# Spectral stage of a two-layer block: the mixing weights of each filter built on GpSimd, with one broadcast product and running sums

## The reference

```python
def _compute_spectral(u, sigma, phi, Mpp, Mpm):
    U_plus, U_minus = _stu_conv(phi, u, PADDED_SL)   # causal convolution with K = 16 filters
    s = sigma ** SIGMA_POW
    out = jnp.einsum('btkd,k,kde->bte', U_plus, s, Mpp)
    out = out + jnp.einsum('btkd,k,kde->bte', U_minus, s, Mpm)
    return out
...
for i, frac in enumerate((1, 2, 4, 8)):
    xi = x[:, :T // frac]
    si = _stu(xi, sigma, phi, M_u[i], M_phi_plus[i], M_phi_minus[i])
    si = jnp.pad(si, ((0, 0), (0, T - si.shape[1]), (0, 0)))
    outs.append(si)
...
return jnp.sum(stacked * weights, axis=-1)
```

## Time and profile before

| | us |
|---|---|
| median of 3 runs | 6255.01 |
| lowest and highest run | 6253.27 and 6257.36 |
| profiled execution, its own time | 6258.71 |
| span of the profiled execution | 6256.9 |
| TensorE products busy in the span | 5702.8 (91%) |
| VectorE busy | 4472.1 (71%) |
| ScalarE busy | 3169.5 (51%) |
| GpSimd busy | 2832.3 (45%) |

### The profile page before, as it was taken

The page is one execution under the profiler, slowest core; times in us unless marked ns, Lnnn a source line. Parts: engine busy times, 40 slices in busy tenths (PEclk is TensorE's granted clock), DMA queues, the critical chain, the costliest instruction groups (busy, mean ns, idle before and its releaser), DMA issues. The chain is left out here.

```text
span 6256.9 us, 128558 instructions
## 1 busy us (share of the span) xinstructions
PE 5702.8 (91%) x41691; PEld 5079.1 (81%) x41691; DVE 4472.1 (71%) x6306; ACT 3169.5 (51%) x6029; POOL 2832.3 (45%) x1695
## 2 busy tenths in 40 slices
PE   7899999999888999999997659999999899999998
PEld 5688888888667888888885538888888788888887
DVE  2699999999618999999995645555555555555554
ACT  2699888988638998899885221111111111111110
POOL 1699999999608999999994300000000000000000
PEclk8899999999989999999999879999999999999999
DMA  2455555555415555555554147776766666777765
GB/s 96 113 141 144 139 142 143 142 143 137 121 56 136 143 143 139 138 145 145 141 138 124 43 128 156 149 152 147 153 151 149 164 140 151 148 154 149 149 150 143
DMA packets 1098945, 858.32 MB, mean 137 GB/s; under 512 B 305622, under 2 KB 1021238, under 8 KB 1064374
## 3 DMA queue, kind: packets, MB, share of 16 engines
q1 hardware_dynamic: 1097974, 844.72, 55.8%
q10 hardware_dynamic: 720, 10.49, 0.4%
HBM read 811.50 MB, written 43.55 MB: 137 GB/s over the span
## 5 line engine op out<-in xcount | busy, mean ns | idle before, releaser
L726 POOL TENSOR_TENSOR read<-state,c_wide 128x1024 f32<-128x1024 f32 x1024 | 2419.3, 2379 | 213.5 <-DVE state L762 127.3
L762 DVE TENSOR_TENSOR_SCAN state<-decay,carry,p_drive 128x512 f32<-128x512 f32 x1792 | 2140.5, 1258 | 104.0 <-PE p_drive L540 57.2
L658 ACT ACTIVATE decay<-step,a_neg 128x512 f32<-128x512 f32 x2048 | 1398.1, 717 | 223.8 <-DVE state L762 214.3
L1747 PE MATMUL p_y<-window,x_high 128*128 128x256 f32 x7936 | 1495.9, 286 | 0.0
L1811 ACT COPY term_blocks<-p_s 128x256 f32<-128x256 f32 x832 | 310.5, 373 | 2157.2 <-PE p_s L1747 2157.2
L1747 PEld LDWEIGHTS p_y<-window,x_high 128*128 128x128 f32 x7936 | 1243.6, 191 | 0.0
L1747 PE MATMUL p_y<-window,x_low 128*128 128x256 f32 x3968 | 1132.5, 285 | 0.0
L553 PE MATMUL p_y<-ident,read 128*128 128x128 f32 x8192 | 1064.1, 273 | 13.0 <-ACT y_tok L672 3.7
L542 PE MATMUL p_drive<-diag_b,xu_tok 128*128 128x128 f32 x8192 | 1002.7, 276 | 1.3 <-DVE state L762 1.3
L542 PEld LDWEIGHTS p_drive<-diag_b,xu_tok 128*128 128x128 f32 x8192 | 959.2, 193 | 1.6 <-DVE state L762 1.6
L553 PEld LDWEIGHTS p_y<-ident,read 128*128 128x128 f32 x8192 | 925.2, 141 | 25.5 <-issue 21.7
(11 more groups left out here) (257 smaller groups left out, 5443.7 us busy)
## 6 DMA issues: line engine op xcount, KB each, us to landing
c_wide<-c_scratch SPq DMA_DIRECT2D x256, 1024.0 KB, 4.8
window<-taps_scratch SPq DMA_DIRECT2D x576, 257.0 KB, 6.4
diag_b<-diag_scratch SPq DMA_DIRECT2D x256, 512.0 KB, 4.1
window<-taps_scratch SPq DMA_DIRECT2D x768, 129.0 KB, 5.1
window<-taps_scratch SPq DMA_DIRECT2D x128, 513.0 KB, 7.3
window<-taps_scratch SPq DMA_DIRECT2D x64, 385.0 KB, 6.2
gate_scratch<-gate_out SPq DMA_DIRECT2D x16, 512.0 KB, 3.1
gate_in<-gate_scratch SPq DMA_DIRECT2D x8, 1024.0 KB, 6.3
```

Source lines behind the costliest of these rows:

```text
L658: act.activation(decay[:, n % 2, t, :], step[:, c.parity, t, :], ACT.Exp, scale=m.a_neg[:, DT2 * c.k + t, n:n + 1]).then_inc(s["decay"], 1)
L726: pool.tensor_tensor(read[:, n % 4, :, :], state[:, n % 4, :, :], wide, ALU.mult).then_inc(s["read_out"], 1)
L762: dve.tensor_tensor_scan(flip(state[:, n % 4, t, :], c), flip(decay[:, n % 2, t, :], c), flip(p_drive[:, n % 2, t, :], c), 0.0 if c.start ...
L1747: last = pe.matmul(out, x[:, source, blk, :], view[:, :, at:at + P][:, :, ::-1], start=first and x is m.x_high and z == 0, stop=True, skip ...
```

## The change

VectorE no longer builds the mixing weights. GpSimd gets its own walk over the filters, with one `build` for the sum and one for the difference. It adds or subtracts the loaded matrices, multiplies all four by their factors in one product, whose second operand is a column of `frac_filter` broadcast along the row, and then makes the running sums with three additions in place. The first step of a filter waits for the loaded matrices, and the first product of a filter waits until the last mix of the filter before is done, since it overwrites `mix_now`. The order of VectorE's other work and the streams of TensorE, ScalarE and SP stay as they are.

```diff
--- before.py
+++ after.py
@@ -1823,30 +1823,38 @@
             act.dma_start(m.acc[:, :, :], m.past_dram[1]).then_inc(s["acc_in"], 16)
             filters(act, 1, body)
 
+        @block.gpsimd
+        def _(pool):
+            def build(n, k, kind):
+
+                if kind == 0:
+                    pool.wait_ge(s["m_in"], START + n * 32 + 32)
+                else:
+                    pool.wait_ge(s["mix_now"], START + n * 2 + 1)
+                pool.tensor_tensor(m_sum[:, :, :], m_both[:, 0, :, :], m_both[:, 1, :, :],
+                                   ALU.subtract if kind else ALU.add).then_inc(s["built"], 1)
+                if kind == 0:
+                    pool.wait_ge(s["mixed"], START + n * 8)
+                pool.wait_ge(s["built"], START + n * 8 + (4 * kind + 1))
+                if kind:
+                    pool.sem_inc(s["m_read"], 1)
+                weight = m.frac_filter[:, :, ds(k, 1)].broadcast_to([P, FRACS, C])
+                pool.tensor_tensor(mix_now[:, kind, :, :], m_sum[:, :, :], weight, ALU.mult).then_inc(s["built"], 1)
+                for r in range(1, FRACS):
+                    pool.wait_ge(s["built"], START + n * 8 + (4 * kind + 1 + r))
+                    ins = pool.tensor_tensor(mix_now[:, kind, r, :], mix_now[:, kind, r, :], mix_now[:, kind, r - 1, :],
+                                             ALU.add)
+                    ins.then_inc(s["built"] if r < FRACS - 1 else s["mix_now"], 1)
+
+            def body(n, k, first):
+                build(n, k, 0)
+                build(n, k, 1)
+
+            for b in range(NB):
+                filters(pool, b, body)
+
         @block.vector
         def _(dve):
-            def sum_weights(n, k, kind):
-
-                if kind == 0:
-                    dve.wait_ge(s["m_in"], START + n * 32 + 32)
-                else:
-                    dve.wait_ge(s["mix_now"], START + n * 2 + 1)
-                dve.tensor_tensor(m_sum[:, :, :], m_both[:, 0, :, :], m_both[:, 1, :, :],
-                                  ALU.subtract if kind else ALU.add).then_inc(s["built"], 1)
-                dve.wait_ge(s["built"], START + n * 8 + (4 * kind + 1))
-                if kind:
-                    dve.sem_inc(s["m_read"], 1)
-                weight = m.frac_filter[:, 0, ds(k, 1)]
-                dve.tensor_scalar(mix_now[:, kind, 0, :], m_sum[:, 0, :], weight, None, ALU.mult).then_inc(s["built"], 1)
-
-            def scale_weights(n, k, kind):
-                for r in range(1, FRACS):
-                    dve.wait_ge(s["built"], START + n * 8 + (4 * kind + 1 + r))
-                    weight = m.frac_filter[:, r, ds(k, 1)]
-                    ins = dve.scalar_tensor_tensor(mix_now[:, kind, r, :], m_sum[:, r, :], weight,
-                                                   mix_now[:, kind, r - 1, :], ALU.mult, ALU.add)
-                    ins.then_inc(s["built"] if r < FRACS - 1 else s["mix_now"], 1)
-
             def with_shared(n, i, to):
 
                 dve.wait_ge(s["kept"], START + n * (SLOTS - 2) + (shared_before(i) + 1))
@@ -1912,10 +1920,6 @@
                     if i == 2:
                         if not first:
                             add(n + -1, 3)
-                    if i in (3, 5):
-                        sum_weights(n, k, (i - 3) // 2)
-                    if i in (4, 6):
-                        scale_weights(n, k, (i - 4) // 2)
                     if i in (3, 4):
                         combine(n, i - 3, 1, 0, 1, ALU.add, i, 0)
                     if i in (5, 6):
```

## The result

The changed kernel takes 6195.4 us (median of 4 runs, 6184.9 to 6197.4) against 6256.2 for the kernel before (median of 4 in the same comparison). The ratio on record is 0.9896, with a 95% interval of 0.9885 to 0.9908; it is estimated from all runs and is not the quotient of the two medians, which is 0.9903. The profiled execution took 6196.9 us with a span of 6195.1, 61.8 less than the profiled one before.

A forecast was written before the change was run, and what follows sets the result against it. TensorE sets the pace, stalled 2.51 us a filter by VectorE's joins; 30 x (2.51 - 0.6 - 0.1 - 0.2) = 48 plus 6 of clock gives 54 us, forecast 6201. Likeliest range 6180 to 6220, eight in ten 6168 to 6232.

The forecast's parts named there:

- The stall: TensorE waiting at slots 9 to 12 for VectorE's joins: 2.51 us a filter, all of it to go.
- GpSimd's cost: Weight building on GpSimd: 9 us a filter, up to 16.4 by upper bounds, hidden in some 27 us.
- a sign of being wrong: GpSimd's small 128x128 additions taking over 0.6 us would show the prediction wrong; 0.40 was taken.
- The port: VectorE's combinations with two SBUF operands wait for GpSimd in slots 3 to 6: about 1.4 us a filter, covered.
- The windows: Loads late next: x at slot 12 by 0.6 us, restart 0.1, w at slot 16 by 0.2, in 30 filters.
- The clock: Seven 3.4 us stretches at half clock in steady filters, about 1.2 us lost in each, 8.6 in all; 6 counted.
- The first filters: First filter of each batch element: TensorE already waits for a window at slot 12, so these two gain nothing.
- What would show it: Spectral stage: VectorE's busy time down about 129 us less stands, combinations 800 to 1000 ns, GpSimd 250 to 300 us.
- The rivals: 1: Window DMAs move up too, so the whole stall and all half-clock stretches go: gain 84 us, 6171; chance 0.13.
- Rival 2: Window DMAs at slots 9 to 16 take nearly all the gain: 0 left, within 0.2%; chance 0.08.
- Rivals 3 and 4: VectorE's port waits give part back, 6231, chance 0.12 (3); or pass 4.03 us a filter, slower, 6297, 0.05 (4).
- Rival 5: GpSimd's weights come late after slot 17; its chain would have to exceed 27 us; no chance given.

The follow-up runs named there:

- e1: Changed kernel with GpSimd building only 4 of 128 columns from the second filter of each batch element on: 6189.7 us, ratio 0.9893.
- e3: Changed kernel with the sum's weights back on VectorE behind joins 3 and 4, the difference's weights still on GpSimd: 6220.2 us, ratio 0.9941.
- e12: As e3, but GpSimd begins the difference's weights only when join 11 is done: 6201.2 us, ratio 0.9903.
- e6: Changed kernel with the second half (low parts of the taps) of windows x, y, w and v not loaded: 6165.8 us, ratio 0.9850.
- e7: Changed kernel with 8 further 128x512 additions of two SBUF operands on GpSimd behind each filter's build: 6281.4 us, ratio 1.0035.
- e4: Kernel before with its weight building still on VectorE, but moved from behind joins 3 to 6 to behind joins 12 to 15: 6192.6 us, ratio 0.9894.
- e2: Kernel before with the new form of the build (broadcast product, three additions) on VectorE in the old places: 6263.5 us, ratio 1.0007.
- e8: Changed kernel with 18 memsets of 128x512 on GpSimd behind each filter's build, reading nothing: 6193.6 us, ratio 0.9893.

## Why the prediction held

The time, 6195.4, lies 6 below the forecast of 6201 and inside both ranges. Step by step:

- **The stall.** Put at 2.51 us a filter, all of it VectorE's. It went wholly and was worth 2.64: 2.54 ahead of slot 12, and 0.10 behind it, since slots 12 to 15 take 11.04 us when slot 12 has waited and 10.94 when it has not. Over 30 filters that is 79 us instead of 75.
- **GpSimd's cost.** Put at 9 us a filter and hidden. Its operations sum to 8.3 (264.5 us in 32 filters), and all but the first sum run from 3921.18 to 3928.92. The start behind the last mix was right, and e1 shows that a filter is no shorter without this work. The product was mis-sized: not 1.27 to 2.37 but 1.05 where nothing stands in its way, below the lower bound. The small additions take 0.57 on average, 0.46 where nothing stands in their way; 0.40 was taken. The rule that the prediction gives for them, a quarter of the large one's streaming time behind a start like the copy's, comes to 0.24 + 0.32 = 0.56 and not to 0.40. At 0.57 they came close to the 0.6 that was named as a sign of being wrong.
- **The port.** Put at 1.4 us a filter, meeting four combinations, and covered. It measured 0.6 on three of them (0.27, 0.19 and 0.13) and is covered, with 0.94 us left at slot 8. That it costs its full size without cover is what e3 and e12 show, there with 1.0 us.
- **The windows.** Put at 0.9 us a filter (0.6 for x, 0.1 restart, 0.2 for w), 27 us. Both places were right: waits stand at slots 12 and 16. The waits view names 14.2 us in the steady filters (21.2 in 20 waits, less 4.9 and 2.1 of the two first filters), but it leaves out the short ones. By the starts of the slots, the 30 filters together come 10 us late to slot 12 (put at 18) and lose 10 at slot 16 (put at 6) and 2 by restarts (put at 3), 22.4 in all. So x was put too high and w too low, and the two errors partly cancel, which is luck. One ordinary filter and the worst one had stood for the spread of x, and 0.6 was too near the worst.
- **The clock.** Seven stretches at 1.2 GHz in steady filters became two, as counted. But a stretch costs 1.47 us (77.04 against 75.57), not 1.2, so the five are worth 7.4 us instead of 6.
- **The first filters.** Put at nothing. The two take 2.7 and 0.8 us longer than before, the second with a new stretch at half clock. The first takes 87.5 to 91.2 us in the runs that load the windows whole and in one part, so this may be chance.

The sum, in us:

| term | forecast | measured |
|---|---|---|
| stall, 30 filters | 75.3 | 79.2 |
| waits for windows and restarts | -27 | -22.4 |
| clock | 6 | 7.4 |
| first filters, start and end of the stage | 0 | -2.6 |
| sum | 54 | 61.6 |

The profiled spans differ by 61.8. The last row but one holds the first filters with 3.5 us, less 0.9 by which the stage begins earlier and its last parts are shorter. No single term explains why the forecast was high: the stall and the windows were each off by some 4 us in the same direction.

**What would show it.** L1899's mean rose to 732 ns, in slots 3 to 5 to 0.81 to 0.95 as said; slot 6 kept 0.68. GpSimd shows 264.5 us, inside 250 to 300. VectorE's busy time fell by 92 us in the stage, not by 129 less some 20. The lengths of its operations did fall by 109; but the recorded spans of neighbouring operations overlap, so an operation that is taken out takes less busy time along than its own length.

The rivals: 1 is e6, which shows that its time is there (6166 against the 6171 worked out) but only if the windows land earlier. Rival 2 did not happen; its sum also takes 0.7 for w where its text says 0.8. Rivals 3 and 4 exist as mechanisms, e3 and e7 show them, but they need GpSimd to read for longer or later than the change does. Rival 5 did not happen: the weights were ready at 3928.92, and no mix waits for GpSimd.

## What to carry to other kernels

Before moving work to an idle engine, look for a later place on the engine that has it. e4 gains as much as the move with two conditions changed, because the work was dear only in the stretch where the consumer waited. After a stall is taken away, the next limit here was the load whose landing time coincides with the new start; it is found by adding issue time and time to landing in the profile of before, and splitting it by who reads which part was worth a further 22 us. In these runs GpSimd work that reads SBUF cost no time only where VectorE was ahead of its consumer or did not work on two SBUF operands just then.

## What the runs showed of the hardware

- GpSimd's 128x512 product with a broadcast column as second operand takes 1.05 us undisturbed, and its addition of two full 128x512 operands 1.27: with the operand that stands still it is cheaper, not dearer. One multiplies and the other adds, and no run separates the two. On VectorE the two cost the same (693 and 682 ns in e2).
- VectorE's two-operand combinations are held up by GpSimd's reads of SBUF and not by its writes. Beside 128x512 additions on GpSimd a pair of combinations takes 2.79 instead of 1.28 us; beside 9.5 us of memsets it stays 1.28. It is mutual: the further additions of e7 average 1567 ns, where an addition of this size alone takes 1.27 us. The Trainium skill (SBUF — State Buffer, section "Who interferes with whom") says this of two-input VectorE instructions, that they contend with a GpSimd instruction that reads SBUF and not with one that only writes it; e7 and e8 agree.
- A stretch of 3.4 us at half the granted clock costs TensorE 1.47 us here: the filters that hold one before the change take 77.04 us, the others 75.57.
